# Opening of a feed-forward block reordered: router ahead of a layer norm, an early square root, channel low parts on VectorE

## The reference, cut to what matters

```python
xn = _layernorm(x)
s = _L0_attn_ref(xn, Wq, Wk, Wv, Wo)                # 16 heads of 64, causal, rotary
# the feed-forward block
routing = softmax(xf @ gate_w.T)                    # xf: 2048 tokens x 1024; gate_w: 8 x 1024
in_scale  = routing @ in_channel_scale              # 8 x 1024
out_scale = routing @ out_channel_scale
out = (xf * in_scale) @ sign(weight).T * out_scale + bias
x = x + s * silu(out)
```

## Time and profile before

| | us |
|---|---|
| median of 3 runs | 1186.87 (1186.68 to 1187.99) |
| time of the profiled execution | 1189.66 |
| its span | 1187.4 |
| TensorE busy in the span | 1142.3 (96%) |
| VectorE busy | 729.4 (61%) |
| ScalarE busy | 616.2 (52%) |
| GpSimd busy | 432.1 (36%) |

### The profile page before, as it was taken

One profiled execution on the slowest core, in us unless ns is written; L12 is line 12 of the kernel. 1 busy time (PEld: TensorE's weight loads), 2 busy tenths in 40 slices (PEclk: granted clock), 3 DMA queues, 4 the chain that ended last, 5 costly groups with the idle time before them and its releaser, 6 DMA issues.

```text
span 1187.4 us, 17857 instructions
## 1 busy us (share of the span) xinstructions
PE 1142.3 (96%) x5736; PEld 954.0 (80%) x5736; DVE 729.4 (61%) x1735; ACT 616.2 (52%) x1291; POOL 432.1 (36%) x258
## 2 busy tenths in 40 slices
PE   4699999999999999999999999999999998999998
PEld 3477777788888888888888888888888886888886
DVE  7676553357776777767767777767767777323133
ACT  5445344155666556656566466655665666322111
POOL 2526427433433424235333343342523523332220
PEclk9799999999999999999999999999999998999999
DMA  6734232302202022021460220202202025555652
GB/s 205 283 107 189 77 107 76 120 0 73 62 9 62 9 71 62 9 62 36 176 212 9 69 59 13 62 9 71 62 9 62 26 72 186 164 182 179 209 196 104
DMA packets 86983, 111.23 MB, mean 94 GB/s; under 512 B 3304, under 2 KB 68840, under 8 KB 85936
## 3 DMA queue, kind: packets, MB, share of 16 engines
q1 hardware_dynamic: 86960, 110.93, 28.7%
HBM read 77.37 MB, written 33.55 MB: 93 GB/s over the span
## 4 chain that ended last, share of the span: by engine, by line
PE 87%; DVE 6%; ACT 3%; POOL 2%; issue 1%; DMA 1%; SPq 0%; DVEq 0%; ACTq 0%; POOLq 0%
PE at_proj L44 17%; PE at_proj L46 17%; PE at_proj L45 17%; PE at_out L909 7%; PE at_pt L896 6%; PE ff_z_ps L264 6%; PE at_score L878 3%; PE at_score L879 3%; PE at_score L44 2%; PE at_score L45 2%; PE at_score L46 2%; PE at_proj L863 1%; POOL ff_xs_lo L601 1%; DMA w_stage<-in_L_ffn_weight_dram 1%; ACT xn_hi L365 1%
## 5 line engine op out<-in xcount | busy, mean ns | idle before, releaser
L44 PE MATMUL at_proj<-xn_hi,w_hi 128*128 128x512 f32 x896 | 363.4, 406 | 2.9 <-ACT at_v_t L1014 2.9
L46 PE MATMUL at_proj<-xn_hi,w_lo 128*128 128x512 f32 x896 | 352.0, 393 | 0.0
L45 PE MATMUL at_proj<-xn_lo,w_hi 128*128 128x512 f32 x896 | 350.8, 392 | 0.0
L46 PEld LDWEIGHTS at_proj<-xn_hi,w_lo 128*128 128x128 f32 x896 | 169.0, 189 | 37.6
L44 PEld LDWEIGHTS at_proj<-xn_hi,w_hi 128*128 128x128 f32 x896 | 169.5, 189 | 33.3 <-issue 3.3
L45 PEld LDWEIGHTS at_proj<-xn_lo,w_hi 128*128 128x128 f32 x896 | 169.8, 190 | 30.4
L1273 POOL TENSOR_TENSOR at_turning<-at_turning,rope_table 128x512 f32<-128x512 f32 x64 | 82.9, 1296 | 305.1 <-DVE at_turning L1144 305.1
L1281 POOL TENSOR_TENSOR w_lo<-w_stage,w_hi 128x1024 fp32r<-128x1024 f32 x45 | 114.5, 2559 | 162.8 <-ACT w_hi L993 162.8
L1031 ACT ACTIVATE at_prob<-at_score,at_neg_max 128x512 f32<-128x512 f32 (+3 forms) x256 | 133.4, 526 | 68.0 <-DVE at_neg_max L1172 67.6
L1040 ACT ACTIVATE at_pt_hi<-at_pt 128x512 fp32r<-128x512 f32 (+1 forms) x192 | 94.0, 524 | 101.1 <-PE at_pt L896 100.4
L1189 DVE TENSOR_TENSOR at_pt_lo<-at_pt,at_pt_hi 128x512 fp32r<-128x512 f32 (+1 forms) x192 | 111.8, 597 | 43.7 <-ACT at_pt_hi L1040 42.8
(11 more groups left out here) (129 smaller groups left out, 1827.7 us busy)
## 6 DMA issues: line engine op xcount, KB each, us to landing
z_store<-z SPq DMA_DIRECT2D x16, 512.0 KB, 2.7
w_stage<-in_L_attn_Wq_dram SPq DMA_DIRECT2D x16, 512.0 KB, 3.8
w_stage<-in_L_attn_Wk_dram SPq DMA_DIRECT2D x16, 512.0 KB, 5.1
w_stage<-in_L_attn_Wv_dram SPq DMA_DIRECT2D x16, 512.0 KB, 6.1
att_store<-at_att_t SPq DMA_DIRECT2D x32, 256.0 KB, 2.0
rope_table<-att_store SPq DMA_DIRECT2D x16, 512.0 KB, 6.5
z<-_attn_hidden_states_dram SPq DMA_DIRECT2D x16, 512.0 KB, 4.5
at_turning<-z_store SPq DMA_DIRECT2D x16, 512.0 KB, 6.1
```

The lines of the kernel that those rows point to most:

```text
L44: pe.matmul(out, sh, mh, start=first, stop=False)
L45: pe.matmul(out, sh, ml, start=False, stop=False)
L46: return pe.matmul(out, sl, mh, start=False, stop=final)
```

## The change

It does four things, all in the opening of `ffn_block`.

1. ScalarE computes the square root for tiles 2 and 3 (`ln_root(2)`) ahead of `x_high(0)` instead of behind it.
2. VectorE runs `sign_copy(3)` and `router(0)` without `layer_norm(4)` ahead of them. `layer_norm(4)` now stands behind `scale(0, 2..3)` and ahead of `scale(0, 4..7)`.
3. ScalarE's `ln_root(4)` moves with it, from behind `sign(3)` to behind `xs_high(0, 0..3)`.
4. `chan_low(0)` and `chan_low(1)` go from GpSimd to VectorE: `chan_low(0)` just ahead of `router(0)`, `chan_low(1)` behind `scale(0, 0..1)`. TensorE's wait for all four of their instructions is split: two ahead of `in_scale(0, 0)`, the other two ahead of the main loop.

```diff
@@ TensorE's program
             route_transposes(0)
-            pe.wait_ge(chan_hi, 2)
-            pe.wait_ge(chan_lo, 4)
+            pe.wait_ge(chan_lo, 2)
             in_scale(0, 0)
             in_scale(0, 1)
             sign_transposes(6)
...
             for i in range(2):
                 pe.wait_ge(sign_copied[i], KT // 2)
+            pe.wait_ge(chan_lo, 4)
             for j in range(BATCH):
@@ ScalarE's program
             sign(1)
+            ln_root(2)
             x_high(0)
-            ln_root(2)
             x_high(1)
...
             sign(3)
-            ln_root(4)
             gate_copy(0)
...
             xs_high(0, range(4))
+            ln_root(4)
             for j in range(BATCH):
@@ VectorE's program
+            def chan_low(c):
+
+                name = ("chan_in", "chan_out")[c]
+                dve.wait_ge(chan_hi, c + 1)
+                for r in (1, 3):
+                    rows = slice(32 * r, 32 * r + 32)
+                    dve.tensor_tensor(keep[name][rows, :], chan_rows[rows, c, :], raw(keep[name][rows, :]),
+                                      ALU.subtract).then_inc(chan_lo, 1)
...
             x_low(3)
-            layer_norm(4)
             sign_copy(3)
+            chan_low(0)
             router(0)
             scale(0, range(2))
+            chan_low(1)
             sign_copy(5)
             sign_copy(7)
             scale(0, range(2, 4))
+            layer_norm(4)
             for j in range(BATCH):
@@ GpSimd's program
-            chan_low(0)
-            chan_low(1)
             xs_low(0, range(4))
```

More of the change, by code:

```diff
@@ L601, in xs_low @@
                     pool.tensor_tensor(xs_lo[:, k, :], xs_full[:, k % 2, :], raw(xs_hi[:, k, :]), ALU.subtract).then_inc(xs_l, 1)
[L603 to L610, removed]
             def z_bias(n):
```

## The result

| | before | changed |
|---|---|---|
| median of the timed executions | 1186.87 (5) | 1191.80 (5) |
| lowest to highest | 1183.62 to 1187.99 | 1189.89 to 1192.47 |
| time of the profiled execution | 1189.66 | 1189.89 |
| its span | 1187.4 | 1187.7 |

The ratio is 1.0043, with a 95% interval of 1.0026 to 1.0061: slower, by 3.1 to 7.2 us. The forecast was +3.2 us; +4.9 us in the medians lies at the very end of its range. The spans of the two profiled executions differ by 0.3 us only. So the pair of traces and the pair of medians tell different sizes, and both have to be explained.

A forecast was written before the change was run, and what follows sets the result against it. TensorE, nearly gapless from tile 4's transposes on, was taken to bound the kernel. Stall 1.1 plus low clock 2.1 gave +3.2 us on the 1186.87 us median: 1190.1 us, range 1186.9 to 1191.8 us.

The forecast's parts named there:

- What bounds the kernel: TensorE is nearly gapless from tile 4's transposes at 58.84 us on; what delays these delays everything behind.
- The slowed layer norm: On VectorE in the opening, layer norm ops wait for GpSimd's subtractions to end, so it runs to 37.2 us.
- Early root: ScalarE's root ahead of the x_high(0) copies: 0.5 us gained, what follows starts 0.5 us earlier.
- Low parts on VectorE: Each table's two subtractions take VectorE 2.3 us (1.216 us each, 0.07 overlap); bounds 2.2 and 2.5 us.
- Layer norm and stall: Unslowed 5.7 us layer norm delays block 4's scale to 53.7; TensorE stands 2.2 us, 1.1 us later than before.
- The sum at the good clock: Shift of tile 4's transposes with TensorE at full clock: +1.1 by TensorE's own path, +1.2 by GpSimd's.
- that path: Block 4's scale, high part, then GpSimd's four low parts to 60.3 us; tile 4's transposes +1.2 against TensorE's +1.1.
- The clock: TensorE's clock is low some 4.4 us after the stall ends at 54.5 us; +2.1 us.
- rival B: Clock stays low about 6 us from thinner TensorE work: 3.0 us lost, +4.1 and more, 1191.0 us up; chance 0.2.
- Rival A: Stall without low clock: it rises before and stays up, or falls briefly; +1.1 to +1.2, 1188.1 us; chance 0.25.
- C: Faster: opening runs at full clock, up to 2.6 us gained, in full -1.5, 1185.4 us; chance 0.12.
- the smaller half: Transposes and input scales of 37 to 46 us at full clock give up to 1.1 us more.
- D: The stall is filled and the change hides all; needs a 3.5 us layer norm; chance counted in C.

The follow-up runs named there:

- e1_norm_back_table_pool: Changed kernel with layer norm and its root back in place, output table's low part on GpSimd behind the router; 1184.72 us, ratio 0.9982 to before.
- e2_norm_moved_only: Kernel before with only the layer norm and its root moved, low parts still on GpSimd; ratio 1.0011 to before.
- e3_changed_third: The changed kernel traced and timed a third time, no edit; 1189.20 us, ratio 1.0016 to before.
- e3_changed_table_pool: Changed kernel with only the output table's low part back on GpSimd, behind the router's end; ratio 1.0013 to before.

## Why the prediction was right or wrong

*What bounds the kernel.* Right. The transposes of tile 4 set the rest, and the rest is the same to 0.6 us in nine of thirteen traces.

*The slowed layer norm.* Right: L501, L503 and L506 are at 0.16, 0.17 and 1.54 us whenever GpSimd is idle, and L501 alone is slow where GpSimd does only the input table. The traces agree in both directions with the exclusive lock of the Trainium skill (SBUF — State Buffer, section "Who interferes with whom"): in the changed kernel the low parts of blocks 0 and 1 took GpSimd 3.11 us instead of the 2.49 of before. The first started at 43.07, while VectorE's output table ran until 43.84; in e1_norm_back_table_pool, without that table on VectorE, the pair takes 2.49 us again.

*Early root.* Right: 0.56 us to `gate(0)`, forecast 0.5.

*Low parts on VectorE.* Too small by 0.2 us each. I took 1.216 us with an overlap of 0.07; two of them took 2.47 us and the next instruction came 0.03 behind. They also cost about 0.1 us of overlap with the instruction ahead of each: 1.26 us from the sign copy to the first instead of 1.13, 1.32 from the scales to the second instead of 1.21. These rows sum to 0.6 us. Transposes and input scale took 2.35 us instead of 2.5.

*Layer norm and stall.* The layer norm took 5.69 us (forecast 5.7), was not slowed and its root waited for VectorE and not for the table. The row of the root lies 2.24 us behind the start of the table load (49.52 to 51.76), 0.97 of it waiting for VectorE: no sign of the drain that the Trainium skill (ScalarE: Activation LUTs, section "What ACT_TABLE_LOAD costs") gives. Nor is there in before: behind the load at 83.19 the next ACTIVATE starts at 84.48, 1.29 us later and without a wait. The scale of block 4 came at 54.44 instead of 53.7, by the two items above and a landing 0.4 us later; TensorE's wait was 1.77 us instead of 2.2.

*The sum at the good clock* was mis-sized. Forecast +1.1 to +1.2; the openings say +1.3 to +1.9 (46.62 and 47.12 against 45.2 to 45.35), the raw difference of the first traces +2.3, with the later landing in it. Two things are missing from it: the dearer low parts, and some 0.5 us in which TensorE, already going again, waits for GpSimd (5.98 us from block 6 to tile 4 instead of 5.44). I had named that path and given it 0.1.

*The clock* is the step that failed. The forecast's +2.1 stood for a clock that is low for 4.4 us behind the stall; that occurred in none of the three traces of the changed kernel. In two the clock came up about when the work ahead of the stall ended, stayed up through the 1.77 us, and the term was nothing. In the third it was low for 6.2 us, which is rival B's length: 8.27 us from block 6 to tile 4 instead of 5.44, +2.8, where B had 3.0. That a stall like this one can be followed by the low clock was right; which case comes, and how long it is low, was not. The rows of before had the rise within 53 to 54 us, close to where the stall would begin. Rival A said so, and the forecast gave it 0.25.

*From the traces to the time.* The prediction added the shift to the median as if both kernels got the same clock behind 60 us. In single executions they don't: 2 us of the first trace of before, and up to 9 us between the lowest and highest times of one kernel. Over the three comparisons the changed kernel was slower by 4.9, 3.2 and 2.1 us. The mean granted clock of its timed executions was 0.984, 0.986 and 0.987 in them, and the mean times 1191.6, 1190.3 and 1189.3 us: the first comparison had the lowest clock. Over the 95 executions of before, 0.001 of clock goes with 0.4 us, so the clock makes an estimated 1.1 us of those 2.4; why the first comparison had the lower clock, and what makes the rest, stays open. The +3.0 us of all executions together lies near the forecast's +3.2, but it is a mean of cases that the forecast had not sized so, and that is luck.

*Rivals.* A occurred twice. B occurred once, in the length of the low stretch and in the opening (+4.2 us); its reason, thinner work of TensorE, is not shown. Of C, the larger half (`gate(0)` at full clock) occurred without the early root and the moved low parts, in e2_norm_moved_only, and a piece of the smaller half, 0.4 us, in e3_changed_third. In e3_changed_table_pool `gate(0)` was slower by 1.1 us instead, so the clock there goes either way. D did not occur: no trace hides the moved layer norm.

## What to carry to other kernels

A wait that an engine has anyway is a place where work costs nothing, and it is lost when the work is taken out of it: the change took the layer norm out of a wait of 6 us that VectorE has anyway and put it where TensorE needed the engine. Before moving a slow piece, ask why it is slow; here it was another engine's work beside it. The two kernels that moved that work out of the way, and kept the output table's part off VectorE, are the two that were shown to be faster (0.2 to 0.3%). And when a change is worth a few us of a thousand, compare a stretch of the trace that ends at the last place it can touch, not two spans, and take more than one trace of each: here three traces of one kernel differed there by 2.9 us.

## What the runs showed of the hardware

- Waits of one and the same length are followed by the lower clock in some executions of a program and not in others: 2.89 us ahead of L44, then 0.77 us for the first matmul in one and 0.47 in another. The rest of the kernel differs by 3.7 us (1124.9 to 1128.6) between the traces with the fewest and the most of such low stretches.
- The clock can come up while TensorE waits, and stay up through a wait: in the changed kernel it was 1.00 over 54 to 55 us, with TensorE idle, and the first matmul behind the wait of 1.77 us took 0.50 us; it took 0.80 in e1_changed_again.
- Some VectorE instructions wait for GpSimd's running instruction to end: those with two inputs in SBUF (L501 1.87 us instead of 0.16, L522 2.11 instead of 0.19), but also TENSOR_SCALAR with one (L503 2.21 us instead of 0.17). TENSOR_REDUCE (L521, 0.19 us) and RECIPROCAL (L499, 0.17) are not held.
- Two subtractions of 32 partitions by 1024 take VectorE 2.47 us and GpSimd 4.8 us.
- The landing of the same early transfer differed by 1.7 us between executions (12.44 to 14.16 us), and the whole opening with it.
